# Reading an attention window's four register values with one load instead of four

## What is computed

```python
# layer 0, 49 windows of 8 x 8 pixels, TOPK = 4, 4 heads of 32 channels
x = x + dwconv3x3(x)
q, k, v = split(layernorm(x) @ qkv_w + qkv_b)
logits = einsum('bpc,bqc->bpq', q_window_means * SCALE, k_window_means)   # 49 x 49 an image
_, idx = top_k(logits, 4)                        # each window: the 4 windows it attends to
k_sel, v_sel = k_windows[idx], v_windows[idx]    # 4 * 64 = 256 keys and values a window
o = softmax(q_window @ k_sel.T) @ v_sel          # a head at a time
x = x + (o + dwconv5x5(v)) @ wo_w + wo_b
x = x + gelu(layernorm(x) @ w1 + b1) @ w2 + b2
# layer 1: 3x3 deformable convolution of an upsampled map, 8 groups x 9 taps,
# sampled at offsets that are computed from x; result = relu(deform) + x
```

## Time and profile before

| | us |
|---|---|
| median of three runs (13882.18 to 13892.24) | 13883.27 |
| the profiled execution, its own time | 13886.23 |
| its span, first to last instruction | 13883.2 |
| TensorE busy | 10537.0 (76%) |
| ScalarE busy | 8917.4 (64%) |
| VectorE busy | 8448.6 (61%) |
| GpSimd busy | 6916.6 (50%) |
| mean granted TensorE clock, share of full speed | 0.918 |

### The profile page before, as it was taken

One profiled execution on the slowest core, in us unless ns is written; L12 is line 12 of the kernel. 1 busy time (PEld: TensorE's weight loads), 2 busy tenths in 40 slices (PEclk: granted clock), 3 DMA queues, 4 the chain that ended last, 5 costly groups with the idle time before them and its releaser, 6 DMA issues.

```text
span 13883.2 us, 501225 instructions
## 1 busy us (share of the span) xinstructions
PE 10537.0 (76%) x187900; PEld 8028.7 (58%) x187900; DVE 8448.6 (61%) x11589; ACT 8917.4 (64%) x18708; POOL 6916.6 (50%) x6167
## 2 busy tenths in 40 slices
PE   3567887878787787878778787877878787741787
PEld 2346665666666666666666666666666666631666
DVE  6446667575666657576666757666675766631743
ACT  1246666667666676766666676666667666741677
POOL 0024554545455454545445454544545454566467
PEclk7679999999999999999999999999999999976999
DMA  4134444445444444444444444444444444431444
GB/s 127 47 78 112 117 113 114 114 109 122 109 117 113 115 116 109 122 110 118 113 116 115 109 121 110 118 111 118 115 109 119 112 118 111 120 75 29 107 128 115
DMA packets 1847066, 1517.08 MB, mean 109 GB/s; under 512 B 1006688, under 2 KB 1381984, under 8 KB 1841568
## 3 DMA queue, kind: packets, MB, share of 16 engines
q1 hardware_dynamic: 1834468, 1474.31, 42.7%
q0 software_dynamic: 9216, 2.38, 0.2%
HBM read 1297.68 MB, written 178.25 MB: 106 GB/s over the span
## 4 chain that ended last, share of the span: by engine, by line
PE 29%; issue 18%; DVEq 12%; ACT 9%; DVE 9%; POOLq 8%; SPq 6%; POOL 6%; DMA 2%; ACTq 1%
PE bank_small L952 6%; DVEq L1478 6%; PE bank_scores L871 5%; PE bank_small L1003 5%; POOLq L658 4%; PE windows L982 4%; DVEq L1463 4%; DVE ol L1479 3%; POOLq L660 3%; POOL gbuf L729 2%; ACT hats L1193 2%; SPq L496 2%; PE bank_post L925 2%; ACT hats L1197 1%; SPq L493 1%
## 5 line engine op out<-in xcount | busy, mean ns | idle before, releaser
L1533 DVE TENSOR_TENSOR prod<-windows,wy 128x640 f32<-128x640 f32 x4032 | 3283.7, 818 | 2036.0 <-PE windows L982 1933.9
L982 PEld LDWEIGHTS windows<-fx,hats 64*64 64x64 f32 x129024 | 2661.1, 139 | 1363.0 <-issue 1292.5
L982 PE MATMUL windows<-fx,hats 64*64 64x80 f32 x129024 | 3293.8, 243 | 181.9 <-issue 148.2
L657 POOL TENSOR_TENSOR prod<-prod 128x768 f32<-128x768 f32 x1344 | 2487.0, 1850 | 1364.8 <-DVE prod L1533 1357.3
L1193 ACT ACTIVATE hats<-hats,cst 128x512 f32<-128x512 f32 x4032 | 2879.1, 714 | 166.6 <-DMA hats<-sample_columns 96.8
L1479 DVE SCALAR_TENSOR_TENSOR ol<-xpad,lepw,ol 128x448 f32<-128x448 f32 x2688 | 2442.1, 909 | 240.9 <-issue 8.0
L1197 ACT ACTIVATE hats<-hats 128x512 f32<-128x512 f32 x4032 | 2517.2, 624 | 6.8
L871 PE MATMUL bank_scores<-ksel,qbd 128*128 128x256 f32 x3136 | 963.7, 434 | 1035.4 <-DVE ob L1464 893.2
L659 POOL TENSOR_TENSOR prod<-prod 128x384 f32<-128x384 f32 x1344 | 1563.0, 1163 | 214.9 <-issue 26.8
L662 POOL TENSOR_TENSOR val<-prod 128x384 f32<-128x384 f32 x1344 | 1497.7, 1114 | 241.1 <-issue 156.2
L952 PE MATMUL bank_small<-wom,ofp 128*128 128x216 f32 x8064 | 1609.4, 355 | 0.0
(11 more groups left out here) (193 smaller groups left out, 13333.4 us busy)
## 6 DMA issues: line engine op xcount, KB each, us to landing
hats<-sample_columns SPq DMA_DIRECT2D x2688, 336.0 KB
ksel<-k_windows SPq DMA_DIRECT2D x3136, 32.0 KB
vsel<-v_windows SPq DMA_DIRECT2D x3136, 32.0 KB
fx<-map_columns SPq DMA_DIRECT2D x64, 420.0 KB
xpad<-in_x SPq DMA_DIRECT2D x17, 1568.0 KB, 13.3
q_windows<-qb SPq DMA_DIRECT2D x112, 224.0 KB, 2.6
k_windows<-kb SPq DMA_DIRECT2D x112, 224.0 KB, 3.5
v_windows<-vb SPq DMA_DIRECT2D x112, 224.0 KB, 3.2
```

The lines of the kernel that those rows point to most:

```text
L657: pool.tensor_tensor(v[:, :, 0:n], v[:, :, 0:n], v[:, :, n:2 * n], ALU.add)
L982: last[h] = pe.matmul(o[m], hat[:, m], fx[XP * h:XP * h + XP, g, row:row + WR, :].rearrange("p r c -> p (r c)"), start=True, stop=True)
L1533: dve.tensor_tensor(o, x, w.unsqueeze(3).to_broadcast([128, 2, CP * WR, CG]), ALU.mult).then_inc(s_wm, 1)
```

## The change

The loop over four `value_load` calls is replaced by one call that loads the four neighbouring numbers into four registers of SyncE. The call is told to leave out the run-time assertion; the bounds 0 and 48 are kept as an assumption. The transfers and their order are the same.

```diff
@@ -489,8 +489,10 @@
                 if w >= NKV:
                     sp.wait_ge(s_pv, cnt(i, HEADS * P2, HEADS * (w - NKV + 1)))
                 hold(sp, "sp")
-                for m in range(TOPK):
-                    v = sp.value_load(sel[0:1, w * TOPK + m:w * TOPK + m + 1], min_val=0, max_val=P2 - 1)
+                _, chosen = nc.values_load_multi_w_load_instructions(
+                    sel[0:1, w * TOPK:(w + 1) * TOPK], engines=[mybir.EngineType.SP], min_val=0, max_val=P2 - 1,
+                    skip_runtime_bounds_check_because="they are places of maxima among P2 logits")
+                for m, v in enumerate(chosen):
                     sp.dma_start(ksel[s][:, m * W2:(m + 1) * W2],
                                  kd[bass.ds(v, 1)].rearrange("a p n -> p (a n)")).then_inc(s_kv[s], 16)
                     sp.dma_start(vsel[s][(m % 2) * 64:(m % 2) * 64 + 64, m // 2, :],
```

## The result

The changed kernel took 13772.65 us at the median of four runs (13738.82 to 13780.41), against 13887.76 us of the kernel before on the same chip: a ratio of 0.9911, 95% interval 0.9896 to 0.9926. It is faster, by 0.7 to 1.0%. The forecast was 13720 us with a range of 13600 to 13830. The direction and the range held; the gain was 115 us where 162 had been worked out. The profiled execution's span went from 13883.2 to 13766.6 us, 116.6 less.

A forecast was written before the change was run, and what follows sets the result against it. No engine bounds the whole; SyncE issues late, uncovered only in an image's first windows. 1.9 + 3.9 + 4.8 = 10.6 us an image, 159 in 15 images plus 3 for the first: 162 off 13886.2, 13720 us, range 13600 to 13830.

The forecast's parts named there:

- SyncE's time a window: SyncE's loads and checks for a window's four numbers: 1.25 to 2.05 us given back, 1.9 taken.
- First scores: Start of an image's attention: TensorE's 4.73 us wait for value sets shrinks by 1.9 us, 2.8 stay.
- First to fourth scores: Next three windows' steps: 31.3 us fall to 27.4, as the second scores' wait goes; 3.9 us an image.
- Fourth to tenth: Six windows with ScalarE's 5.50 us column wait: 66.8 us fall to 62.0, as where SyncE caught up; 4.8 us.
- Tenth to last: The other 39 windows of an image: 2.7 us gain at most, 0 taken.
- Most of the lag stays: Rival: wide load costs four and first waits are transfers' landing, so only the start gains; 13825 to 13865 us, chance 0.14.
- The steady part shrinks too: Rival: tenth to last scores shorten and the clock no longer drops, up to 21 us an image; 13570 us, chance 0.10.
- SyncE the true bound: Rival: all 49 windows give 1.9 us, 93 us an image; 12490 us, chance 0.02.
- Slower, by denser transfers: Rival: closer transfers delay the column group behind two map transfers, twice an image; 165 us lost, 14020 us, chance 0.04.
- SyncE's waits above 50 us: Sign: in 490 us of an image's attention SyncE waits above 50 us instead of 3.2.
- the sum of waits below 80: Sign: whole-kernel waits of TensorE's scores for values and ScalarE for columns fall from 216.8 to below 80 us.
- the clock above 0.90: Sign: TensorE's granted clock in the stretch behind an image's first scores rises above 0.90, from 0.86.

The follow-up runs named there:

- fixed_places: Kernel before with constant places instead of the four numbers read, so no loads, checks or top-k selection: 13318.57 us, whole time not comparable; period 792.2 us.
- columns_early: Changed kernel with a column group issued ahead of the first window's transfers, these one slot later, and half the first queries behind them: 13728.02 us, ratio 0.9879.
- the repeat: The changed kernel run once more without an edit, as a control: 13747.61 us against 13900.92 of the kernel before, ratio 0.9893.
- the repeat of before: The kernel before profiled once more without an edit, as a control: 13890.2 us in one run.
- loads_twice: Kernel before with a second load and its checks added for each of a window's four numbers: 15353.44 us, ratio 1.1056.

## Why the prediction was right, and where its sum was off

**SyncE's time a window.** 1.9 us was taken, between 1.25 and 2.05. Read directly it is 7.5 - 5.8 = 1.7 us (1.5 by the medians, 7.4 and 5.9): inside the bounds, below the value taken. The load of four took 476 ns where about 0.3 us was expected, and three key issues a window took 0.1 us more each: 2.05 - (0.476 - 0.268) - 0.3 = 1.5. The Trainium skill's rule ("Runtime: NRT & Kernel Launch", "Instruction fetch mechanics") of some 200 ns for each register even in bulk did not hold for this load from SBUF: 268 ns for one number, 476 for four. Of what the prediction drew from that rule, one thing came true all the same, by another road: the dropped assertions are the larger part of the change, 1.1 of 1.7 us.

**First scores.** 1.9 us expected, 18.2 - 16.8 = 1.4 measured. The step was right, and its size is what SyncE saves in an image's first window: 7.8 us before, 6.4 now. The wait that stays was to be 2.8 us and was 2.8 (39.4 us in 14 images). In `fixed_places`, with no load at all, 28.0 / 14 = 2.0 us of it are left: most of this wait is the pairs' issue and landing, not the load.

**First to fourth scores.** 3.9 expected, 31.1 - 28.5 = 2.6 measured. Of the three gains this one was most mis-sized. The 27.4 us put together from later steps of the same kinds were not reached. The second scores' wait did not quite go: 7.9 us in 11 images are left of 38.4 in 15, and the first step takes 8.8 us instead of 8.3. And the 8.0 us taken for the third step were those of one image; its mean is 8.5, before as after, so there was nothing to gain. `columns_early`, with 27.0, reaches such a sum by a first step of 7.4.

**Fourth to tenth.** 4.8 expected, 66.3 - 60.9 = 5.4 measured, nearly all of it in one step, from the seventh to the eighth scores (13.6 to 8.5). The waits of ScalarE for columns behind the map transfers, 76.8 us in 14 images, fell to 5.8 us in 6. The comparison with images in which SyncE was ahead gave the size well.

**Tenth to last.** 0 expected, 2.0 us lost (405.4 to 407.4; 407.3 in the repeat, 405.8 in the repeat of before). This is the step that failed in sign: 1.5 to 2.0 us in 15 images are 25 to 30 of the 45 us between forecast and result. One such mean is uncertain by 0.6 to 1.0 us, since the images of one profile lie some 10 us apart, but all eleven profiles of relieved kernels, by no load, fewer checks or another order, lie above both of before, at 406.4 to 408.4 (together 407.3 against 405.6). About half of it, 1.0 us, lies at one place, the interval between the scores of windows 29 and 30 (10.5 us in both profiles of before, 11.5 and 11.8 in the changed kernel, 11.1 to 11.9 in the other relieved kernels). The map transfers of slot 144 stand there. Before, SyncE issued them 16.7 us behind the scores of window 28, after GpSimd had left its branch on the samples' reach. The timeline of that stretch in one image (TensorE, GpSimd, SyncE, VectorE):

```profile
4582.50 1.10 PE L871 MATMUL bank_scores<-ksel,qbd 128*128 128x256 f32 x4 [1.49 <-DVE ob L1464]
...
4595.66 0.38 POOL L638 TENSOR_SCALAR pxy<-pxy 128x72 f32<-128x72 f32 x1 [4.11 <-issue]
...
4599.18 1.94 SPq L551 DMA_DIRECT2D fx<-map_columns  x2
...
4600.84 0.63 DVE L1493 TENSOR_TENSOR yw<-t 128x448 f32<-128x448 f32 x1 [1.97 <-ACT t L1160]
```

In the changed kernel they are issued 3.3 us behind those scores, ahead of the branch:

```profile
4530.26 1.86 PE L873 MATMUL bank_scores<-ksel,qbd 128*128 128x256 f32 x4 [1.95 <-DVE ob L1466]
...
4533.52 1.94 SPq L553 DMA_DIRECT2D fx<-map_columns  x2
...
4547.60 0.39 POOL L640 TENSOR_SCALAR pxy<-pxy 128x72 f32<-128x72 f32 x1 [6.64 <-issue]
...
4550.26 1.15 DVE L1495 TENSOR_TENSOR yw<-t 128x448 f32<-128x448 f32 x1 [2.62 <-ACT t L1162]
```

GpSimd's stop at the branch grew from 4.11 to 6.64 us, its sums then fall beside VectorE's next steps, and the step shown takes 1.15 us instead of 0.63. Over the 13 images SyncE issues these transfers 15.1 us behind the scores of window 28 before and 3.8 now, and the stop is 3.2 us and 6.8; VectorE's steps of this line in the interval take 0.63 and 0.70 us in the two profiles of before and 0.76 to 0.95 in the relieved kernels, less of a difference than in the image shown. In all other relieved kernels the transfers are early (2.7 to 5.5 us) and the stop is long (5.6 to 7.3). This goes together in every profile but was not tried alone: the other part of the loss, and that the transfers ahead of it are what slows the branch, stay open.

**The sum.** 1.4 + 2.6 + 5.4 - 2.0 = 7.4 us an image and 0.6 in the other parts make 8.0; over the span, 116.6 / 8.0 = 14.6 images, where 15 were counted. Expected were 10.6. The pair of repeats has 803.5 - 794.2 = 9.3, so a good part of the distance to the forecast is within what the runs differ by. One sum of the range does not come out: 1.25 us a window and half of the middle terms are 1.25 + 4.35 = 5.6 us an image, 84 us in 15, not 60. The upper end would have been some 25 us lower, and the result lies inside it either way.

**The rivals.** Most of the lag stays: no, 62.0 of 216.8 us of waits are left. But in time the result lies about halfway between the forecast and this rival's 13825, in part because of what was given back (the repeat lies nearer the forecast). The steady part shrinks too: no, it grew by 2.0 us. SyncE the true bound: no, though `loads_twice` shows how near it was. Slower, by denser transfers at the map transfers of slot 72: no, ScalarE's wait for columns there fell to 5.8 us in all. Something was given back at another place (slot 144), where the transfers now come earlier, at a lower price: up to 30 us in all where the rival had 165, and by what mechanism is open.

**What was to be seen.** SyncE's waits above 50 us (64.3), the sum of waits below 80 (62.0), the clock above 0.90 (0.92): right. The first scores' wait at 2.8 us: right. The waits of the second scores and of ScalarE's columns: nearly gone (7.9 and 5.8 us left), that of the fifth gone. From the tenth scores on 405 us as before: wrong, 407.4. The load near 0.3 us or at 0.8: 0.476, nearer to the first but neither.

## What to carry to other kernels

An engine that issues transfers can be late without being the bound: it has no waits of its own, and the others wait for it only where its buffers have no lead. A saving there pays at those places and not in every window. Here the first 1.1 us a window (the assertions) gave 7 us an image and the last 1.1 (all that is left of loads and address steps) 2 to 3, while 2.2 us added made the engine the bound and cost 94: some eight times as much for each us as was won by taking away.

To see what each half of a change is worth, set its gain beside the engine's own time for it. The assertions gave the larger part of the gain because they were the larger part of SyncE's time.

## What the runs showed of the hardware

- A load of four neighbouring numbers from SBUF into registers took 476 ns at the median. A load of one took 268; in the kernel before, the first of a window's four took 453 and the others 267 (medians, worked out from its timeline). So four numbers cost about as much as the first load of a window.
- A check of a register's bounds on SyncE took 152 to 159 ns for the register instruction and 18 for the assertion. Dropping four of them took 1.1 us off SyncE's time, some 0.28 each with the hand-over, whether they stood between the transfers or ahead of them.
- The issue of a key transfer of 32 KB with an address from a register took 346 to 351 ns at the median where a load stood ahead of each pair of transfers (with checks or without), and 439 to 444 where none did. So part of what is taken from between transfers comes back in their issue.
- One more wait and mark a window on TensorE, always met, cost 3 to 5 us an image by the runs, and in the profile it did so at a place where they do not stand (slots 0 to 29 of the loop's passes behind a jump back), with TensorE idle for no cause that the profile names. The same kind of wait on ScalarE cost nothing there.
